# VectorE's jobs, bank copies and the branch on the maxima, moved between the steps of a head attention

## What is computed

```python
def _L1_xattn_ref(q, k, v, Wq, bq, Wk, bk, Wv, bv, Wo, bo):
    NUM_HEADS = 16; D_K = 8
    qh = _split_heads(q @ Wq + bq)
    kh = _split_heads(k @ Wk + bk)
    vh = _split_heads(v @ Wv + bv)
    scores = jnp.einsum('bhsd,bhtd->bhst', qh, kh) / np.sqrt(D_K)
    attn = jax.nn.softmax(scores, axis=-1)
    out = jnp.einsum('bhst,bhtd->bhsd', attn, vh)
    return out @ Wo + bo
...
x = x + _L1_xattn_ref(_layernorm(x, axis=-1), ctx_1024, ctx_1024, ...)
```

## Time and profile before

| | us |
|---|---|
| median of 3 runs | 2137.61 (2137.54 to 2146.88) |
| profiled execution | 2143.8 |
| its span | 2142.0 |
| ScalarE busy, PE busy, VectorE busy | 1329.8, 1788.6, 1064.8 |
| head attention, first to last exponential | 739.0 to 1640.4 |

### The profile page before, as it was taken

How to read it: one execution, slowest core, us unless ns; L and a number is a source line. 1 busy time by engine, 2 the same in 40 slices (tenths; PEclk the granted TensorE clock), 3 DMA queues, 4 the chain that set the end, 5 groups by cost and what they waited for, 6 DMA issues and landing times. The chain is left out here.

```text
span 2142.0 us, 48718 instructions
## 1 busy us (share of the span) xinstructions
PE 1788.6 (83%) x19832; PEld 1148.4 (54%) x19832; DVE 1064.8 (50%) x2767; ACT 1329.8 (62%) x1479; POOL 255.1 (12%) x191
## 2 busy tenths in 40 slices
PE   2447999999999288888888888888886499999998
PEld 2336998998997144444444444444443245455554
DVE  5897222222222434444444444444442677777773
ACT  0003444444443088888888888888886266666675
POOL 7722000000001200000000000000000012221122
PEclk9667999999999599999999999999998599999999
DMA  7211000000000233333333332333220100000000
GB/s 228 52 19 42 1 1 2 1 1 2 1 1 1 57 85 65 76 76 76 74 73 73 72 71 58 72 68 69 59 60 4 56 1 6 6 5 6 5 5 10
DMA packets 37525, 87.82 MB, mean 41 GB/s; under 512 B 11705, under 2 KB 24514, under 8 KB 36802
## 3 DMA queue, kind: packets, MB, share of 16 engines
q1 hardware_dynamic: 34242, 78.53, 15.4%
q0 software_dynamic: 3072, 6.30, 1.6%
HBM read 32.59 MB, written 2.10 MB: 16 GB/s over the span
## 5 line engine op out<-in xcount | busy, mean ns | idle before, releaser
L1194 ACT ACTIVATE C_probs<-C_ps_s 128x1024 f32<-128x1024 f32 x832 | 777.2, 1044 | 147.9 <-PE C_ps_s L1112 147.9
L1125 PE MATMUL C_ps_o<-C_probs,C_values 128*16 128x256 f32 x6656 | 456.1, 393 | 41.1 <-DVE C_o_t L1340 23.7
L1655 ACT ACTIVATE D_hidden<-D_ps_u,D_b_up 128x1024 f32<-128x1024 f32 x256 | 275.4, 1114 | 151.8 <-PE D_ps_u L1571 151.7
L698 ACT ACTIVATE B_hidden<-B_ps_h,B_b_up 128x512 f32<-128x512 f32 x288 | 194.3, 688 | 188.9 <-PE B_ps_h L626 187.0
L1112 PE MATMUL C_ps_s<-C_queries,C_keys 32*128 32x256 f32 x3328 | 217.9, 337 | 71.3 <-ACT C_probs L1194 51.1
L639 PE MATMUL B_ps_e<-B_w_down,B_hidden 128*128 128x128 f32 x2304 | 275.4, 276 | 0.0
L639 PEld LDWEIGHTS B_ps_e<-B_w_down,B_hidden 128*128 128x128 f32 x2304 | 270.5, 192 | 8.4
L1125 PEld LDWEIGHTS C_ps_o<-C_probs,C_values 128*16 128x16 f32 x6656 | 155.7, 97 | 189.6 <-ACT C_probs L1194 46.6
L1112 PEld LDWEIGHTS C_ps_s<-C_queries,C_keys 32*128 32x128 f32 x3328 | 131.2, 189 | 209.4 <-ACT C_probs L1194 144.1
L793 DVE SCALAR_TENSOR_TENSOR B_acc<-B_ps_e,B_gate,B_acc 128x128 f32<-128x128 f32 x224 | 63.1, 345 | 289.1 <-PE B_ps_e L639 289.1
L1571 PE MATMUL D_ps_u<-D_up_in,D_w_up_r 128*128 128x512 f32 x512 | 186.6, 446 | 2.5 <-ACT D_hidden L1655 1.2
(11 more groups left out here) (260 smaller groups left out, 2023.7 us busy)
## 6 DMA issues: line engine op xcount, KB each, us to landing
C_keys<-C_k_hi SPq DMA_DIRECT2D x128, 200.1 KB, 4.3
C_ctx_t<-ctx_t_dram SPq DMA_DIRECT2D x16, 800.5 KB, 4.4
C_keys<-C_k_lo SPq DMA_DIRECT2D x64, 200.1 KB, 4.2
C_queries<-C_q_hi SPq DMA_DIRECT2D x128, 32.0 KB, 2.1
B_w_up<-L_ffn_w_up_dram SPq DMA_DIRECT2D x1, 2304.0 KB
B_w_down<-L_ffn_w_down_dram SPq DMA_DIRECT2D x1, 2304.0 KB, 26.6
A_ids<-ids_dram SPq DMA_DIRECT2D x1, 2048.0 KB, 13.3
C_queries<-C_q_lo SPq DMA_DIRECT2D x64, 32.0 KB, 2.3
```

The lines of the kernel that those rows point to most:

```text
L698: nc.scalar.activation(hidden[:, e % HB, c, :], ps_h[c][:], ACT.Gelu, bias=b_up[:, u:u + 1]).then_inc(s_hid, 1)
L1125: m = T.matmul(ps_o[32 * j:32 * j + 2 * DK, g % 2, :], values[:, parity, kt, g * HG + j, :], probs[:, slot(parity, 2 * step + j // 2), j % ...
L1194: nc.scalar.activation(probs[:, slot(parity, n)], ps_s[bank(parity, n)][:], ACT.Exp, scale=SCORE_SCALE1).then_inc(s_exp, 1)
L1655: nc.scalar.activation(hidden[:, u % RING, :, :], ps_u[u % 2][:], ACT.Gelu, bias=b_up[:, u % PAIRS:u % PAIRS + 1]).then_inc(s_hid, 1)
```

## The change

The tables are renumbered, and five things move. (1) The copies of the output bank stand one step earlier on VectorE, in steps 1 and 14, ahead of the job and the reciprocal of that step. (2) The two normalizations stand ahead of the job of step 5. `turn` moves from step 8 to 7, and `split_keys` stands behind it. Step 8 has no job. (3) The `query` job signals after `q_t`; a value job comes between `query` and `bound`, and `bound` waits for a semaphore of its own, `s_bound`. (4) The branch of the maxima moves from step 22 to step 14, which has no job; it now waits for the first 13 jobs (`PREPARED`). The job behind it, a value job in step 15, waits on TensorE for `s_top_read`, which VectorE gives after its branch. (5) The output projection moves from steps 15 to 18 to steps 16 to 19, the adding to the stream from 19 to 20, and the last four value jobs from 19 to 22 to steps 20 to 23.

```diff
-        JOBS = ([("key", i) for i in range(len(KEY_AT))] + [("turn", 0), ("query", 0), ("bound", 0), ("count", 0)]
-                + [("value", i) for i in VALUES])
+        VALUE_JOBS = [("value", i) for i in VALUES]
+        JOBS = ([("key", i) for i in range(len(KEY_AT))] + [("turn", 0), ("query", 0)] + VALUE_JOBS[:1]
+                + [("bound", 0), ("count", 0)] + VALUE_JOBS[1:])
...
-        JOB_AT = {u: n for n, u in enumerate((*range(7), *range(8, 15), *range(19, 23)))}
+        JOB_AT = {u: n for n, u in enumerate((*range(8), 9, 10, 11, 12, 13, 15, *range(20, 24)))}
...
-        FIN_AT = {15: 0, 16: 1, 17: 2, 18: 3}
-        INVERT_AT = {10: 0, 11: 1, 12: 2, 13: 3}
-        ADD_AT = 19
+        XN_AT = 5
+        SPLIT_AT = 7
+        INVERT_AT = {10: 0, 12: 1, 13: 2, 14: 3}
+        MAXIMA_AT = 14
+        PREPARED = sum(1 for u in JOB_AT if u < MAXIMA_AT)
+        FIN_AT = {16: 0, 17: 1, 18: 2, 19: 3}
         FIN_AFTER = sum(1 for u in JOB_AT if u < min(FIN_AT))
-
-        TAKE_AT = {LAG: 1, SPAN + LAG: 0}
-        MAXIMA_AT = 22
+        ADD_AT = 20
+
+        TAKE_AT = {LAG - 1: 1, SPAN + LAG - 1: 0}
...
                     elif kind == "bound":
+                        pe.wait_ge(s_bound, p + 1)
...
-                            pe.wait_ge(s_top_read, TOP_READS * (k + 1) + 1)
+                            if first:
+                                pe.wait_ge(s_top_read, TOP_READS + 1)
...
                         if n in JOB_AT and not last:
+                            if JOB_AT[n] == PREPARED:
+                                pe.wait_ge(s_top_read, TOP_READS * (k + 2) + 1)
...
-                            maxima(k + 1, 1 - parity, turn + parity)
+                            maxima(k + 1, 1 - parity, turn + parity, PREPARED)
...
-                        chain.step(V.tensor_scalar(q_t[:], ps_p[:, 0:SEQ], bqk[:, 0:1], None, ALU.add))
+                        V.tensor_scalar(q_t[:], ps_p[:, 0:SEQ], bqk[:, 0:1], None, ALU.add).then_inc(s_job_done, 1)
+                        dve.wait_ge(s_job_done, NJ * p + n + 1)
...
-                        done = V.tensor_scalar(q_bound[:], q_bound[:], ends[:, 3:4], None, ALU.mult)
+                        V.tensor_scalar(q_bound[:], q_bound[:], ends[:, 3:4], None, ALU.mult).then_inc(s_bound, 1)
...
                     for n in range(STEPS):
+                        if n == XN_AT and not last:
+                            normalize(k + 1)
...
+                        if n == SPLIT_AT and not last:
+                            split_keys(1 - parity, turn + parity, False)
+                        if n == MAXIMA_AT and not last:
+                            maxima(k + 1, 1 - parity, turn + parity, PREPARED)
                         if n in INVERT_AT and not first:
                             invert(k - 1, INVERT_AT[n])
-                        if n == MAXIMA_AT and not last:
-                            maxima(k + 1, 1 - parity, turn + parity)
```

## The result

| | before | after |
|---|---|---|
| median of the runs, us | 2142.24 (4 runs, 2137.54 to 2147.10) | 2057.22 (4 runs, 2052.62 to 2058.59) |
| profiled execution, its span, us | 2143.8, 2142.0 | 2056.1, 2054.3 |
| exponentials of ScalarE: idle time before them, us | 147.9 | 65.0 |
| the same: busy time, us | 777.2 | 772.3 |

The ratio after to before is 0.9614, with a 95% interval of 0.9588 to 0.9639; the medians lie 85 us apart. The table of the kernel before its change gave the median of three of these runs, 2137.61; the fourth took 2147.10, and the median of all four is 2142.24.

The account below looks back on a forecast made before the run. ScalarE's exponentials bound the kernel, with 113.4 us of gaps inside the rounds; 33 us would remain, 80.4 less, so 2143.8 becomes 2063.4 profiled and 2057.2 in the median. Forecast 2050 to 2066 (chance 0.48); eight in ten, 2038 to 2084.

Parts of the forecast that it names:

- Normalization, bound, first copy: In the middle rounds, ScalarE's gaps of 1.48, 0.67 and 1.55 us at these three places were to go.
- The cluster of step 14: Behind the copy and branch in step 14, step 17 starts 1.5 us late a round (1.2 to 1.9).
- The clock behind step 14: TensorE's clock falls behind step 14's standings in nine of 14 rounds, 0.7 us a round (0 to 2.0).
- The heads of rounds: Waits at the heads of rounds go, with 4 to 5 us of cover; 0.6 us at the last round's head.
- Round 0: First round, no reciprocals and no projection in step 14: 0.8 us there, and 0.4 remain of the start.
- The 6.2: The median was put 6.2 us lower than the profiled execution, 2057.2 against 2063.4.
- (a): Step 14 cheaper, 0.7 to 1.2 us a round, no clock fall: 2039, or 2047 with branch 1.5; chance 0.22.
- (b): Second copy and branch stay in series, gaps 1.06 and 1.32 remain, clock falls as often: 2069 or 2081; chance 0.20.
- (c): SP's key placing heads the round, each us over 31 costing 14, 2098 at 8 over; chance, with other partial losses, 0.05.
- (d): Slower: the clock falls in step 14 and stays low, 2243 if through steps 14 to 22; chance 0.03.
- (e): No change: the gaps reappear at unseen places, in the same sum; chance 0.02.
- the part on the splitting: Key splitting, 3.71 us, starts 2.15 into step 7, ends 0.35 into step 10; 0.2 us cover for the value job.

Follow-up runs that it names:

- The four undoings near the old places: Normalization, first copy, bound or branch each put back alone in the changed kernel, at or near its old place: 2091.7, 2078.4, 2068.7 and 2066.95 us.

## Why the prediction was right, step by step

**The total was right, 2057.2 against 2057.2, and so near by luck: it hides errors that cancel.** The mechanism was right: the old gaps go, and one smaller cluster behind step 14 takes their place. The sum of idle time inside the rounds was forecast as 33 us (32.6 before rounding), and 30.4 were found:

- *Normalization, bound, first copy:* all three gaps gone as argued, nothing new in their place. The undoings gave +34.5, +11.5 and +21 us. The clock's falls behind the transposes went with the gap; the trace of before has six more low stretches that the prediction did not count, four behind the branch (from 1140.3 for one) and two at heads of rounds, and these are gone as well. The close covers held: `query` came in time for step 10's value job, and no gap stands ahead of `count`.
- *The cluster of step 14:* forecast 1.5 us a round (1.2 to 1.9), found 1.7, 3.4 us more over 14 rounds. The steps up to the clearing were right within 0.07 us (copy 2.07 and 2.14, clearing 2.74 and 2.75, `weigh` 2.85 and 2.88). The step that failed is the next: "From the clearing to its signal ... I take 1.5", with bounds of 1.19 and 1.94; in the round shown it was 2.10, above both, and about 2.0 in the median of 14. Those bounds came from a branch with no large transfer beside it. The term itself was good, 1.42 to 1.80 with the keys' transfers left out; what I missed is that the move puts the branch among them.
- *The clock behind step 14:* forecast 0.7 us a round, 9.8 in all, found nought. I had taken the frequency of the transposes, nine in 14, for a cluster in which the idle times of TensorE's weight loads are single ones of 0.90, 0.65, 1.38 and 0.72 (together 3.65 us within 6.1). The Trainium skill, TensorE: Matmul & The Clock Gate, "Loop structure matters more than you think", says that a copy out of PSUM by VectorE doesn't break TensorE's warmth, and after's trace agrees (granted clock 1.0 there). But the kernel with the late second copy shows that this isn't so of every such wait: there TensorE stood 4.26 us for a copy of VectorE, and the granted clock was 0.53. In these traces the falls go with the length of one standing, though not strictly. By the idle time of the weight loads, the clock fell behind all 14 standings of 3.8 to 5.2 us (the late second copy), behind nine of 14 of 2.26 (the transposes of rounds 1 to 14 of the kernel before), behind four of 15 of 1.8 to 2.0 at the branch and two of seven of 1.81 at heads in the same kernel, and behind none of 14 of 1.81 at its first copy. After has single standings of up to 1.82 in the rounds and no fall. Why one standing of 1.8 us is followed by a fall and another isn't stays open. My error was to add up short standings and give their sum the frequency of one long one. The stretch behind the branch of round 6 in the kernel before, clock at 0.57:

```profile
1140.00:1144.00 4.00, 4.00 (x48) 1.64 (x48) 0.00 (x0) 3.55 (x5) 0.00 (x0) 0.57 0.44 138
```

- *The heads of rounds:* forecast 0.6 for one, found 0.68 seven times, 4.8 us. I had said that a gap at a head would prove me wrong; it does for this step, though the gap is the old one, which the earlier trace rows don't show apart from the clock's, and not a wait for SP. The placing of the keys did not become the head, as forecast: SP waited 193 us in all for `k_lo` in after, and its waits no longer show one for the maxima.
- *Round 0:* 1.2 us forecast (0.8 and 0.4), 1.2 found.
- *The ends of runs:* 4.9 us of ScalarE's busy time, of which the sum had nothing. With it the profiled span would have been forecast 5 us lower.

Together: 3.4 (cluster) + 4.8 - 0.6 (heads) - 9.8 (clock) is 2.2 less, and the ends of runs take off another 4.9, so the profiled execution came to 2056.1 instead of 2063.4. The median, which I had put 6.2 below the profiled execution, is 1.1 above it. The 6.2 was chance in the choice of the profiled execution and in having three runs: with the fourth the median of before lies only 1.6 below its profiled execution. Without that step the same sum would have said 2061.8 to 2063.4, still inside the stated range. So the 7.3 us that the sum missed were made good by chance.

**Rivals.** (a) was right that the clock doesn't fall, and wrong that VectorE's branch takes 1.19 us: from the clearing to the value job it was 1.44 at the least. Its 2047 with a branch of 1.5 missed for the slow load; with the keys' transfers left out the kernel does run in 2048, though the heads of rounds (4.8 us) and the ends of runs (4.9) make part of that agreement chance. (b) would have needed both old gaps; the series it feared exists only with the copy behind the branch. (c), (d) and (e) did not occur. In (c) the price and the amount don't fit: at 14 us for each us over 31, 8 us over make 112, and its 2098 needs 3; the 8 fit about if counted from the 26.3 of the estimate. In the part on the splitting its end is put 0.35 us into step 10, where 2.15 + 3.71 - 5.58 gives 0.28; nothing hangs on it.

**How far the parts add.** The four undoings near the old places give 34.5 + 21 + 11.5 + 10 = 77 us of 85 by the medians, and 35.8 + 23.8 + 10.5 + 9.7 = 79.8 of the 82.9 us by ScalarE's idle time. That they come so near the whole isn't proof that the parts are independent: undoing the normalization also shortens the load of the flag, which hides 6.6 us of its price. The second copy's old place was not tried by itself, since in step 15 it now falls behind the branch.

Left open: what TensorE does at the head of every second round (its weight loads idle for 1.81 us, ScalarE for 0.68), and why the load of one number from the tile takes longer beside the large transfers. That the two come together is shown, not how.

## What to carry to other kernels

When a step is moved, ask what its hidden small operations will run beside in the new place, not only whether its time fits: a register load of 0.3 us became one of up to 1.2 beside large transfers, and the cure was not to make it faster but to have no job wait for it. Before a copy that frees a bank, keep the engine free of long operations; here two reciprocals moved by a step gave 12 us. And when the clock is in the sum, weigh the longest single standing of TensorE, not the idle time of a stretch.

## What the runs showed of the hardware that I had not expected

- VectorE's load of a number into a register took 0.30 to 0.32 us in 15 of 16 cases of the kernel before, and 0.32 to 1.23 us in after, beside transfers of 200 KB; beside the queries' transfers of 32 and 128 KB alone it stayed at 0.30 to 0.32.
- TensorE standing 4.26 us for a copy of VectorE came back at half speed (`weigh` 1.91 us instead of 1.06), and was at full clock again within some 5 us of starting. It was so in all 14 rounds, while in the kernel before a low clock followed four of 15 standings of 1.8 to 2.0 us at the branch.
- Four standings of 0.65 to 1.38 us within 6.1 us left the clock at 1.0.
- Exponentials in a row come every 0.92 us, and the last one of a run takes 0.1 us more, so each interruption costs that beyond its gap.
